# The PSUM bank of a block's layer norms is put into its attention's ring of two, which becomes a ring of three

## The reference, cut to what matters

```python
def _L0_attn_ref(x, ln_g, ln_b, w_qkvb, b_qkvb, w_out, b_out):
    mu = jnp.mean(x, axis=-1, keepdims=True)
    var = jnp.mean((x - mu) ** 2, axis=-1, keepdims=True)
    normed = (x - mu) * lax.rsqrt(var + LN_EPS) * ln_g + ln_b
    q, k, v, beta_pre = jnp.split(normed @ w_qkvb + b_qkvb, 4, axis=-1)
    beta = jax.nn.sigmoid(beta_pre)
    ...
    k = k / jnp.maximum(jnp.linalg.norm(k, axis=-1, keepdims=True), NORM_EPS)
    def step(S, inp):
        q_t, k_t, v_t, beta_t = inp
        retrieval = jnp.einsum('bhij,bhj->bhi', S, k_t)
        S = S + jnp.einsum('bhi,bhj->bhij', beta_t * (v_t - retrieval), k_t)
        return (S, jnp.einsum('bhij,bhj->bhi', S, q_t))
    ...
def _L0_ffn_ref(x, w1_w, w1_s, w2_w, w2_s, h1_w, h1_s, h2_w, h2_s, w3_w, w3_s):
    h = jax.nn.silu(_tlin(x, w1_w, w1_s)) * _tlin(x, w2_w, w2_s)
    h = jax.nn.gelu(_tlin(h, h1_w, h1_s), approximate=False)
    h = jax.nn.gelu(_tlin(h, h2_w, h2_s), approximate=False)
    return _tlin(h, w3_w, w3_s)
x = x + 0.5 * _L0_ffn_ref(_layernorm(x), ...)
x = x + _L0_attn_ref(_layernorm(x), ...)
x = x + 0.5 * _L0_ffn_ref(_layernorm(x), ...)
```

## Time and profile before

| | us |
|---|---|
| median of 3 runs | 1817.11 |
| lowest and highest | 1815.38, 1817.98 |
| the profiled execution | 1814.47 |
| its span, first to last instruction | 1812.8 |
| TensorE's matmuls busy, x10030 | 1729.3 (95%) |
| TensorE's weight loads busy, x10030 | 1068.9 (59%) |
| VectorE busy, x2890 | 1242.2 (69%) |
| GpSimd busy, x1501 | 1208.6 (67%) |
| ScalarE busy, x2115 | 1055.7 (58%) |

### The profile page before, as it was taken

How to read it: one execution, slowest core, us unless ns; L and a number is a source line. 1 busy time by engine, 2 the same in 40 slices (tenths; PEclk the granted TensorE clock), 3 DMA queues, 4 the chain that set the end, 5 groups by cost and what they waited for, 6 DMA issues and landing times.

```text
span 1812.8 us, 29738 instructions
## 1 busy us (share of the span) xinstructions
PE 1729.3 (95%) x10030; PEld 1068.9 (59%) x10030; DVE 1242.2 (69%) x2890; ACT 1055.7 (58%) x2115; POOL 1208.6 (67%) x1501
## 2 busy tenths in 40 slices
PE   6989989999999999999999999999999999999999
PEld 5855555555555555555555555578655555555588
DVE  5255776777776877868767687777776768777331
ACT  4656555474656565656556474656656555655454
POOL 4463876767676767777676667667776767675653
PEclk9999999999999999999999999999999999999999
DMA  7100000000000000000000000000000000000000
GB/s 289 44 1 1 1 1 1 1 1 2 0 1 1 24 1 24 1 1 1 1 2 1 1 24 1 1 25 1 1 1 1 1 1 13 1 1 12 1 13 13
DMA packets 5270, 23.16 MB, mean 13 GB/s; under 512 B 640, under 2 KB 1664, under 8 KB 3584
## 3 DMA queue, kind: packets, MB, share of 16 engines
q1 hardware_dynamic: 5120, 21.26, 3.2%
HBM read 17.06 MB, written 4.19 MB: 12 GB/s over the span
## 4 chain that ended last, share of the span: by engine, by line
PE 65%; DVE 10%; issue 8%; POOL 8%; ACT 7%; POOLq 0%; ACTq 0%; DVEq 0%
PE ffn_bank L1083 40%; PE ffn_bank L1066 5%; PE att_bank L1131 5%; PE att_bank L1103 4%; POOL hid_lo L565 3%; PE state_bank L1139 2%; PE att_bank L1118 2%; POOL pairs_lo L602 2%; PE ln_bank L1024 2%; PE att_bank L1119 2%; POOL pairs L594 2%; ACT hid L680 2%; DVE hid L821 1%; ACT L680 1%; DVE terms L920 1%
## 5 line engine op out<-in xcount | busy, mean ns | idle before, releaser
L1083 PE MATMUL ffn_bank<-hid_hi,w_sb 128*128 128x512 f16 (+1 forms) x2736 | 905.9, 346 | 7.8 <-ACT gate L667 4.6
L1083 PE MATMUL ffn_bank<-hid_lo,w_sb 128*128 128x512 f16 (+1 forms) x2736 | 905.8, 346 | 0.0
L565 POOL TENSOR_TENSOR hid_lo<-hid,hid_hi 128x512 f16<-128x512 f32 (+1 forms) x456 | 462.7, 1030 | 296.2 <-ACT hid_hi L656 295.9
L594 POOL TENSOR_TENSOR pairs<-KQ 128x32 f32<-128x32 f32 (+15 forms) x496 | 325.7, 667 | 123.8 <-DVE KQ L848 104.8
L1083 PEld LDWEIGHTS ffn_bank<-hid_hi,w_sb 128*128 128x128 fp8e4 x2736 | 275.9, 101 | 206.5 <-issue 11.3
L1083 PEld LDWEIGHTS ffn_bank<-hid_lo,w_sb 128*128 128x128 fp8e4 x2736 | 268.6, 98 | 205.7 <-issue 12.4
L602 POOL TENSOR_TENSOR pairs_lo<-pairs,pairs_hi 128x448 f16<-128x448 f32 (+15 forms) x416 | 313.0, 757 | 74.0 <-ACT pairs_hi L728 73.7
L728 ACT CAST pairs_hi<-pairs 128x448 f16<-128x448 f32 (+15 forms) x416 | 174.8, 438 | 158.9 <-POOL pairs L594 157.6
L656 ACT CAST hid_hi<-hid 128x512 f16<-128x512 f32 (+1 forms) x456 | 234.9, 552 | 30.7 <-DVE hid L821 30.0
L680 ACT ACTIVATE hid<-ffn_bank,par_sb 128x512 f32<-128x512 f32 (+1 forms) x304 | 171.7, 616 | 123.5 <-PE ffn_bank L1083 122.8
L1066 PE MATMUL ffn_bank<-xn_hi,w_sb 128*128 128x512 f16 (+1 forms) x532 | 177.6, 348 | 9.1 <-DVE hid L821 6.6
(11 more groups left out here) (92 smaller groups left out, 2134.9 us busy)
## 6 DMA issues: line engine op xcount, KB each, us to landing
NK<-in_w SPq DMA_DIRECT2D x11, 1024.0 KB, 5.9
X<-in_x SPq DMA_DIRECT2D x7, 512.0 KB, 3.6
out<-X SPq DMA_DIRECT2D x7, 512.0 KB, 2.6
wqkvb_sb<-in_wqkvb SPq DMA_DIRECT2D x1, 1024.0 KB, 8.6
X<-in_x SPq DMA_DIRECT2D x2, 256.0 KB, 6.5
out<-X SPq DMA_DIRECT2D x2, 256.0 KB, 2.1
wout_sb<-in_wout SPq DMA_DIRECT2D x1, 256.0 KB, 9.3
par_sb<-in_par SPq DMA_DIRECT2D x1, 24.0 KB, 2.5
```

The costliest lines, as they stand in the source:

```text
L565: pool.tensor_tensor(hid_lo[layer % 2][:, m, call.cols], hid[:, u % HID_BUFFERS, call.cols], hid_hi[layer % 2][:, m, call.cols], ALU.subtr ...
L594: pool.tensor_tensor(packed(pair(pairs, q, dot), n), later, earlier, ALU.mult).then_inc(pairs_made if dot in SPLIT else pairs_ready, 1)
L1083: mm = nc.tensor.matmul(ffn_ps(call, j), weight(name, kk, 2 * pair + i), v[:, kk, cols], start=kk == 0 and part == 0, stop=kk == KT_FF - 1 ...
```

## The change

The layer norms' bank goes away and the attention's ring has three banks. Both sums of every norm become uses of the ring (`("ln", i, "mean")` and `("ln", i, "var")`), at the place in `USES` where TensorE issues them, and take a bank in turn. The list holds 726 uses, 70 of them sums of norms. The reader of a mean is VectorE's `center`, that of a variance ScalarE's `root`. Since readers now read in another order than TensorE fills, `READ_AT` holds each reader's tick and turn, and `READ` counts in that order. The semaphores `ln_filled` and `ln_read` are replaced by `att_filled`, `att_read_v` and `att_read_s`. `LN_ATT` and the other tables of the norms, with `JOBS`, stand further up in the file and are otherwise as they were; line numbers of the changed file are higher by 18 to 19 on TensorE.

```diff
-ATT_BANKS = 2
+ATT_BANKS = 3
...
+SAVE_LAG = 2
+USES, WHEN, READ_AT = [], {}, {}
+
+
+def add_use(use, tick, turn):
+
+    USES.append(use)
+    READ_AT[use] = (tick, turn)
+
+
+for _job in JOB_HEAD:
+    for _n, _part in enumerate(("mean", "var")):
+        add_use(("ln", _job.i, _part), -2 * TICKS + 2 * _job.i + _n, 0)
 for _f in FRAMES:
     for _e in range(FIRST_TICK if _f < 0 else 0, TICKS):
+        for _job in JOBS_IN[_f]:
+            for _part, _reader in (("mean", "center"), ("var", "root")):
+                if _job.ticks[_part] == _e:
+                    add_use(("ln", _job.i, _part), _f * TICKS + _job.ticks[_reader], 0)
         if _f + 1 < PARTS:
-            USES += [("proj", _f + 1, _which) for _which in E_PROJ if E_PROJ[_which] == _e]
+            for _which in E_PROJ:
+                if E_PROJ[_which] == _e:
+                    add_use(("proj", _f + 1, _which), _f * TICKS + _e + 1, 2)
             if _e == E_NORM:
-                USES.append(("norm", _f + 1, 0))
+                add_use(("norm", _f + 1, 0), _f * TICKS + _e + 1, 3)
         if 0 <= _f < PARTS and _e in E_RETR:
-            USES.append(("retr", _f, E_RETR.index(_e)))
-        USES += dots_at(_f, _e)
-        WHEN.update({dot: _f * TICKS + _e for dot in dots_at(_f, _e)})
+            add_use(("retr", _f, E_RETR.index(_e)), _f * TICKS + _e + SAVE_LAG, 1)
+        for _dot in dots_at(_f, _e):
+            add_use(_dot, _f * TICKS + _e + 1, 2)
+            WHEN[_dot] = _f * TICKS + _e
         if _f >= 1 and _e == E_OUT:
-            USES.append(("out", _f - 1, 0))
+            add_use(("out", _f - 1, 0), _f * TICKS + _e + 2, 1)
 U = {use: j for j, use in enumerate(USES)}
-READER = {"proj": "S", "norm": "S", "retr": "S", "kk": "V", "qk": "V", "out": "V"}
+READER = {"proj": "S", "norm": "S", "retr": "S", "kk": "V", "qk": "V", "out": "V", "mean": "V", "var": "S"}
 READ = {}
 for _reader in "SV":
-    READ.update({use: 1 + i for i, use in enumerate(u for u in USES if READER[u[0]] == _reader)})
+    _own = [u for u in USES if READER[u[2] if u[0] == "ln" else u[0]] == _reader]
+    READ.update({use: 1 + i for i, use in enumerate(sorted(_own, key=lambda u: READ_AT[u]))})
 DOTS = [use for use in USES if use[0] in ("kk", "qk")]
 DOT = {use: q for q, use in enumerate(DOTS)}
 SPLIT_FROM = {"kk": 6, "qk": 0}
...
-        ln_bank = bank("ln_bank")
...
-        ln_summed, ln_filled, ln_read, ln_squared, ln_sq_summed, ln_inverted, ln_normed = (sem(n) for n in (
-            "ln_summed", "ln_filled", "ln_read", "ln_squared", "ln_sq_summed", "ln_inverted", "ln_normed"))
+        ln_summed, ln_squared, ln_sq_summed, ln_inverted, ln_normed = (sem(n) for n in (
+            "ln_summed", "ln_squared", "ln_sq_summed", "ln_inverted", "ln_normed"))
...
-                    act.wait_ge(ln_read, i * 2 + 1)
+                    act.wait_ge(att_read_v, READ["ln", i, "mean"])
                     act.activation(xn[:, :, cols], xc[:, :, cols], ACT.Square).then_inc(ln_squared, 1)
                 if part == "root":
-                    act.wait_ge(ln_filled, i * 2 + 2)
+                    act.wait_ge(att_filled, U["ln", i, "var"] + 1)
+                    ps = bank_of("ln", i, "var")
                     if job.kind == "att":
-                        act.activation(roots[:, 1, cols], ln_bank[:, 0:n], ACT.Sqrt, bias=eps[:, 1:2])
-                    act.activation(roots[:, 0, cols], ln_bank[:, 0:n], ACT.Sqrt, bias=eps[:, 0:1]).then_inc(ln_read, 1)
+                        act.activation(roots[:, 1, cols], ps[:, 0:n], ACT.Sqrt, bias=eps[:, 1:2])
+                    act.activation(roots[:, 0, cols], ps[:, 0:n], ACT.Sqrt, bias=eps[:, 0:1]).then_inc(att_read_s, 1)
                 if part == "apply":
                     act.wait_ge(ln_normed, i + 1)
                     if job.kind == "att":
...
-                    dve.wait_ge(ln_filled, i * 2 + 1)
-                    nc.vector.tensor_tensor(xc[:, :, cols], slab(job.s, cols), both(ln_bank[:, 0:n]), ALU.subtract).then_inc(ln_read, 1)
+                    dve.wait_ge(att_filled, U["ln", i, "mean"] + 1)
+                    nc.vector.tensor_tensor(xc[:, :, cols], slab(job.s, cols), both(bank_of("ln", i, "mean")[:, 0:n]), ALU.subtract).then_inc(att_read_v, 1)
                 if part[:5] == "recip":
                     quarter = part[5:]
                     if quarter in ("", "0"):
-                        dve.wait_ge(ln_read, i * 2 + 2)
+                        dve.wait_ge(att_read_s, READ["ln", i, "var"])
...
                 if part == "mean":
                     pe.wait_ge(ln_summed, i + 1)
-                    if i:
-
-                        pe.wait_ge(ln_read, i * 2)
                 if part == "var":
                     pe.wait_ge(ln_sq_summed, i + 1)
                 if part in ("mean", "var"):
-                    nc.tensor.matmul(ln_bank[:, 0:cols.stop - cols.start], average[:, :], feature_sum[:, cols], start=True, stop=True).then_inc(ln_filled, 1)
+                    ps = att_use("ln", i, part)
+                    nc.tensor.matmul(ps[:, 0:cols.stop - cols.start], average[:, :], feature_sum[:, cols], start=True, stop=True).then_inc(att_filled, 1)
...
             def att_use(*use):
                 i = U[use] - ATT_BANKS
                 if i >= 0:
-                    pe.wait_ge(att_read_v if READER[USES[i][0]] == "V" else att_read_s, READ[USES[i]])
+                    before = USES[i]
+                    pe.wait_ge(att_read_v if READER[before[2] if before[0] == "ln" else before[0]] == "V" else att_read_s, READ[before])
                 return bank_of(*use)
...
```

More of the change, by code:

```diff
@@ L159, in dots_at, with ffn_ln, half_ln @@
     return found + [("qk", f - 1, t) for t in range(C) if E_QK[t] == e and 1 <= f <= PARTS]
-USES, WHEN = [], {}
+QUARTERS = 4
+def ffn_ln(at):
+    return dict(sum=at, mean=at + 4, center=at + 5, square=at + 6, sq_sum=at + 7, var=at + 11, root=at + 11,
+                recip0=at + 12, recip1=at + 13, recip2=at + 14, recip3=at + 15, norm=at + 19, apply=at + 20, low=at + 22)
+def half_ln(at):
+    return dict(sum=at, mean=at + 2, center=at + 3, square=at + 4, sq_sum=at + 5, var=at + 7, root=at + 8,
+                recip0=at + 8, recip1=at + 9, recip2=at + 10, recip3=at + 11, norm=at + 13, apply=at + 14, low=at + 15)
@@ new lines, with add_job @@
+LN_ATT = dict(sum=18, mean=22, center=24, square=25, sq_sum=27, var=30, root=32, recip=35, norm=37, y_recip=38, apply=38, low=39)
+LN_SECOND = dict(sum=26, mean=30, square=32, sq_sum=36, var=40, root=43, apply=62, low=66)
+LN_FFN = [(-1, 55), (0, 55), (1, 52), (2, 55), (4, 52), (5, 55), (6, 55), (7, 55), (8, 55), (9, 55), (10, 55), (11, 49), (12, 50), (13, 55), (14, 55), (15, 55), (16, 54)]
+JOBS = []
+def add_job(kind, part, call, frame, ticks):
+    atts = sum(j.kind == "att" for j in JOBS)
+    if kind == "att":
+        job = Job(len(JOBS), kind, part, part // HALVES, None, atts, slice(part % HALVES * HALF, (part % HALVES + 1) * HALF), frame, ticks)
+    else:
+        job = Job(len(JOBS), f"ffn{call.which}", None, call.s, call.n, atts, call.cols, frame, ticks)
+    JOBS.append(job)
+    return job
@@ new lines @@
+JOB_HEAD = [add_job("ffn", None, CALLS[0], None, None), add_job("ffn", None, CALLS[1], None, LN_SECOND)]
+for _f in FRAMES:
+    if _f + 1 < PARTS:
+        add_job("att", _f + 1, None, _f, LN_ATT)
+    for _anchor in [a for f, a in LN_FFN if f == _f]:
+        _call = CALLS[[j.kind != "att" for j in JOBS].count(True)]
+        add_job("ffn", None, _call, _f, ffn_ln(_anchor) if _call.weight == 2 else half_ln(_anchor))
+JOBS_IN = {f: [j for j in JOBS if j.frame == f] for f in FRAMES}
+SAVE_LAG = 2
@@ L734, in attention @@
                     for c in range(HCH):
-                        if e == E_RETR[c] + 2:
+                        if e == E_RETR[c] + SAVE_LAG:
                             save_q(f, c)
```

27 lines of the change are left out of this document (removed).

## The result

| | before | after |
|---|---|---|
| median, us (4 runs each) | 1816.42 | 1806.2 |
| lowest and highest | 1815.38, 1817.98 | 1805.1, 1807.16 |
| the profiled execution | 1814.47 | 1805.1 |
| its span | 1812.8 | 1803.4 |

The ratio of the times is 0.9944, with a 95% interval of 0.9933 to 0.9956: 10.2 us less by the medians, 9.4 us less in the profiled executions. The forecast was 1810.9 us, with a range of 1804.5 to 1817.0.

What follows compares the result with a forecast made beforehand. TensorE was taken as the bound, with 12.9 us of direct bank waits. Kept terms 2.45 + 0.47 + 1.25 + 2.05 = 6.2 us, off the median 1817.11 us, gave 1810.9 us, range 1804.5 to 1817.0.

Steps and rivals of the forecast that it cites:

- The bound: Whole run: TensorE sets the end; its direct waits for a bank of the attention's ring of two come to 12.9 us.
- Nothing moves: On every engine instructions, their number and order stay; only waits change, and the semaphore edits cost nothing.
- the added waits, 0: 35 more waits on variance sums and 68 uses waiting for a norm's reader: cost 0, at least 0.9 us to spare.
- 309, 4.2 us gone, 2.45 kept: TensorE's stop at 309 for ScalarE's save and the low clock behind it: 4.2 us go, 2.45 us are kept.
- 510.13 and the three of its kind: At 510.13 0.74 us go, 0.47 us kept before a transpose; three other waits for VectorE's taking keep 1.25 us.
- The terms set to 0: At 505.31, 599.6 with 607.90, ScalarE's projection wait and 418.81: freed time returns at the next late thing; 0 kept.
- The small ones, 2.05 us: 31 short bank waits, 2.9 us in all: 0.85 us lost to late GpSimd or VectorE, 2.05 us kept.
- rival C: Slower: returning waits gather, at 611.64 or six other places, lowering the clock; 1.65 us per fall, some 1821 us; chance 0.04.
- What I named as signs: Bank waits, the 309 stop and its low clock go; waits for transposes and GpSimd's differences grow about 5 us together.
- A: Everything is kept: VectorE and GpSimd follow TensorE everywhere; gain 14.6 us, 1802.5 us; chance 0.07.
- B: Nearly nothing is kept: 309 shrinks to under 1 us, small waits drown; gain 0 to 3 us, around 1815.5; chance 0.26.
- norm turns would take the third bank's worth: Norm sums, 70 of 726 uses, leave the ring as deep as before for 164 uses; part of the 0.26 chance.

Runs made afterwards that it cites:

- run 3: Changed kernel, three banks with norms in the ring, but each attention use also waits for the reader two attention uses before: 1815.72 us, ratio 1.0003 to the kernel before.
- run 5: Changed kernel with norm sums in the ring but only two banks, one left idle: 1833.91 us, ratio 1.0108 to the kernel before.
- run 11: Changed kernel with the old waits put back on products of keys only, all other uses freed: 1811.25 us, ratio 0.9976 to the kernel before.
- run 1: The kernel before once more, no edit, for a second trace: 1815.76 us.
- run 2: The changed kernel once more, no edit: 1805.52 us, ratio 0.9951 to the kernel before.
- run 10: Changed kernel with the norms of frames 1 and 4 starting one tick later (anchors 53): 1805.17 us, ratio 0.9944 to the kernel before.
- run 9: Kernel before, two banks, norms of frames 1 and 4 one tick later so ScalarE's cast follows the save: 1810.64 us, ratio 0.9976.
- run 7: Kernel before with ScalarE's save of each retrieval's queries one tick earlier: 1828.68 us, ratio 1.0068.
- run 8: Changed kernel with ScalarE's save of each retrieval's queries one tick earlier: 1822.98 us, ratio 1.0043 to the kernel before.
- run 4: Changed kernel with the old waits put back except on products of keys of row 8: 1811.26 us, ratio 0.9982 to the kernel before.
- run 6: Changed kernel with the old waits put back except on all products of keys: 1811.6 us, ratio 0.998 to the kernel before.

## Why the prediction was right, and where its sum was off

**The bound.** Right. Idle time of TensorE for want of a bank was what could be won, and run 3 shows that nothing else of the change counts.

**"Nothing moves" and the added waits, 0.** Right for three banks (run 3, ratio 1.0003), and the row that I looked for is the one that appears with two (run 5).

**309, 4.2 us gone, 2.45 kept.** 4.04 us went, 2.67 were kept. The size holds; what is late next was misnamed, so that 2.45 and 2.67 lie so close is in part luck. GpSimd's difference at 310.51 takes 1.09 us back first, and the update behind the transpose only 0.3.

**510.13 and the three of its kind, 0.47 and 1.25.** 0.58 and 1.29.

**The terms set to 0** (505.31, 599.6 with 607.90, 1482.7, 414). All four within 0.1 us of 0: 5.3 us of idle time and hidden parts went there, and nothing was kept. VectorE's 17.28 of 18 us busy had said so for the largest. Where it comes back was right at 505 and 1482.7 only: at 414 it is at the next product of keys (0.55 us) and not at 418.81, and at 599 to 611 in front of the feed-forward and not at the transpose. The argument that a release is worth only what the next late thing allows is the step of this prediction that paid.

**The small ones, 2.05 us: the term that was mis-sized.** They kept 2.96 us in this trace, and the complement in run 11 bears it out. I had counted only places where the load starts 0.05 to 0.13 us behind the reader, 2.9 us in all, and struck 0.85 us for places where GpSimd or VectorE is late next. So either the 0.85 us were not lost, or there are more short waits than the 31 that I found; the runs don't say which.

**The clock: a term that was missing.** I counted the fall that goes at 309, and weighed new ones (rival C). I did not see that falls of the unchanged program also differ from run to run. The fall at 1193, in a stretch without bank waits, gives 1.56 us of the 9.38, half of the 3.2 us by which the sum of 6.2 fell short. It is told below. The mean clock of each execution says more than one trace. In the traces six stretches at 1.2 GHz go with a mean of 0.994 (run 1), four with 0.996 (before), three with 0.997 (after) and two with 0.998 (run 2), so one stretch is about 0.001. The kernel before has 0.9948 over the 54 executions beside the runs, the changed kernel 0.9970 over 9: about two stretches fewer, of which the one at 309 is only one. So on the average a second one goes too, and what it gives (1.56 us at 1193, nothing at 103) is part of the measured difference. Which one goes and why stays open, and run 10 reaches the same time with 0.9956.

**What I named as signs.** The bank waits and the stop at 309 went as said. TensorE's waits for transposed values and for GpSimd's differences did not grow by about 5 us: they grew by 0.1 and 0.2 (`Uz` and `pairs_lo`). The 4.8 us that came back stand mostly in front of the feed-forward and of the products of keys in full precision. I had also called the 68 uses that follow a norm sum by three places attention's; the list of uses has 50 of attention among them and 18 variance sums. That changes no term.

**The whole.** The measured 1806.2 us lie within the range, 4.7 below the forecast. The gain was 10.2 us by the medians, a little over the 3.6 to 10 that the forecast's chance stood for.

**The rivals.** A would have given 14.6 us, and falls with the four zeros. B falls with the result (the interval is 8 to 12 us) and with runs 2 and 3. C falls: TensorE's clock was lower in four stretches before and in three after, the one that is new at 103 lies far from the places named, and the waits that came back at 599 to 611 stayed below 1 us each. That norm turns would take the third bank's worth is refuted by the gain.

With the old waits the ratio is 1.0003, without them 0.9951 (runs 3 and 2): a bank more gave 0.5%, since matmuls waited for one by the rows. The Trainium skill ("TensorE: Matmul & The Clock Gate", section on HAM oscillation) tells of a kernel where double-buffering PSUM gave nothing further; this case does not follow it.

## What to carry to other kernels

A ring of PSUM banks that is shared by readers on two engines is as slow as the one reader that stands behind a foreign wait in its own queue. Look at that queue first: moving one operation past the other (run 9) gave half of what a bank gave, 2.5 us of it at this place, though moving the wrong one cost 14 and 17 us (runs 7 and 8). For the sum, follow each removed wait to the next thing that is late and keep only what it allows, and count the many waits that are too short to have a row: here they were 3 of 7.5 us.

## What was not expected of the hardware

**The same stop, with and without a fall of the clock.** In every trace TensorE stands still for 2.38 or 2.39 us at 1185 to 1209, for ScalarE's gate, behind the same matmuls. Before, and in the run of the change with moved anchors (run 10), the step of a 256-column matmul afterwards is 0.21 us, and in the kernel after 0.11:

```profile
1192.77 0.37 PE L1083 MATMUL ffn_bank<-hid_hi,w_sb 128*128 128x256 f16 x1 [2.38 <-ACT gate L667]
1192.94 0.42 PE L1083 MATMUL ffn_bank<-hid_lo,w_sb 128*128 128x256 f16 x1
1193.15 0.42 PE L1083 MATMUL ffn_bank<-hid_hi,w_sb 128*128 128x256 f16 x1
```

```profile
1187.07 0.27 PE L1101 MATMUL ffn_bank<-hid_hi,w_sb 128*128 128x256 f16 x1 [2.38 <-ACT gate L687]
1187.17 0.27 PE L1101 MATMUL ffn_bank<-hid_lo,w_sb 128*128 128x256 f16 x1
1187.28 0.27 PE L1101 MATMUL ffn_bank<-hid_hi,w_sb 128*128 128x256 f16 x1
```

The first fence is the kernel before, the second the one after. The clock was at 1.2 GHz behind this stop in nine traces (before, runs 1, 3, 4, 7 to 11) and at 2.4 GHz in four (after, runs 2, 5 and 6); each fall cost 1.5 to 1.7 us where it stood, though that at 103 was made up by shorter waits behind it. The length of the stop does not tell them apart. So a difference of 1.5 us between two profiled executions can be the clock alone.

**A stretched VectorE instruction.** The product of 128 x 512 (`norm` of an attention's layer norm) runs 22 times in each of the 13 traces. One of them takes 3.4 us in every trace, at 1094 in that of before. At about 1254 it took 0.82 us in the trace of before and 3.20 us in run 11, as in five other traces (runs 1, 4, 6, 7, 8), the kernel before itself among them (run 1). First the trace of before, VectorE's row between GpSimd's:

```profile
1254.58 1.31 POOL L565 TENSOR_TENSOR hid_lo<-hid,hid_hi 128x256 f16<-128x256 f32 x2
1255.61 0.82 DVE L808 TENSOR_TENSOR xn<-xc,roots 128x512 f32<-128x512 f32 x1
1255.84 1.62 POOL L602 TENSOR_TENSOR pairs_lo<-pairs,pairs_hi 128x512 f16<-128x512 f32 x1
```

Then run 11:

```profile
1252.53 1.30 POOL L584 TENSOR_TENSOR hid_lo<-hid,hid_hi 128x256 f16<-128x256 f32 x2
1253.55 3.20 DVE L828 TENSOR_TENSOR xn<-xc,roots 128x512 f32<-128x512 f32 x1
1253.79 1.16 POOL L621 TENSOR_TENSOR pairs_lo<-pairs,pairs_hi 128x512 f16<-128x512 f32 x1
1254.90 1.30 POOL L584 TENSOR_TENSOR hid_lo<-hid,hid_hi 128x256 f16<-128x256 f32 x2
```

In run 11 the product ends 0.55 us after GpSimd's last row; in the trace of before it ends 0.55 us after GpSimd's first, and there it is GpSimd's next instruction that is longer (1.62 us against 1.16). The same shows in all 286 of these products. The 154 that begin while GpSimd runs nothing take 0.68 or 0.69 us. Each of the other 132 ends 0.55 us after an instruction of GpSimd: 109 after the one that was running (they take 0.76 to 1.37 us), 23 after the second, fourth or fifth of instructions without a gap (1.7 to 3.4 us). So by these rows GpSimd's instructions hold the product up. Which of the two goes first when a GpSimd instruction ends stays open, and no run was made for it.

At 1258 the stretched product delays a projection by 1.95 us. It is why medians and ratios, not traces alone, decide between runs 4, 6, 9 and 11, which lie within 1 us of each other.
